# Adding beta on VectorE, an earlier request for raw weights, and a new order in the half tiles of a 1-core attention and mixture-of-experts kernel

## What is computed

```python
xn = _layernorm(x)
Q, K, V = xn @ Wq + bq, xn @ Wk + bk, xn @ Wv + bv        # 16 heads; Q and K have two halves of 64
A1, A2 = Q1 @ K1.T * s, Q2 @ K2.T * s                     # 512 x 512 for each batch and head
P = softmax(A1) - lam * softmax(A2)
Y = concat(P @ V) @ Wo + bo
attn = (layernorm(Y) * gamma + beta) * (1.0 - 0.8)
logits = t @ switch_w + switch_b                          # t: the 4096 tokens of xn; 8 experts
out = gelu(t @ w1[e] + b1[e]) @ w2[e] + b2[e]             # e = argmax of the logits, for each token
x = x + attn + out * max(softmax(logits))
```

## Time and profile before

| | |
|---|---|
| Median of 3 runs | 1838.65 us (1837.49 to 1839.98) |
| The profiled execution | 1841.33 us, of which the span of the trace is 1839.5 us |
| PE, DVE, ACT, POOL busy in the span | 97%, 84%, 77%, 36% |
| Front stage | to about 1465 us; PE full from 80 us on |
| Feed-forward stage | about 1465 to 1726 us; half tiles from 1652 us |
| Output stage | about 1726 us to the end |

### The profile page before, as it was taken

How to read it: one execution, slowest core, us unless ns; L and a number is a source line. 1 busy time by engine, 2 the same in 40 slices (tenths; PEclk the granted TensorE clock), 3 DMA queues, 4 the chain that set the end, 5 groups by cost and what they waited for, 6 DMA issues and landing times. The chain is left out here.

```text
span 1839.5 us, 32514 instructions
## 1 busy us (share of the span) xinstructions
PE 1789.6 (97%) x10474; PEld 1392.6 (76%) x10474; DVE 1538.1 (84%) x2636; ACT 1409.6 (77%) x3358; POOL 663.9 (36%) x717
## 2 busy tenths in 40 slices
PE   5999999999999999999999999999999999999997
PEld 4777777777777777777777777777677699999997
DVE  3988898899889888988898889888999866887467
ACT  4898888888888888888888888888788776676422
POOL 2444222222222222223222222222237455556554
PEclk8999999999999999999999999999999999999899
DMA  7899988888888888888888888888877586667698
GB/s 232 228 247 251 247 226 220 224 236 219 218 226 237 224 222 228 233 223 218 235 232 214 212 234 225 220 218 231 227 206 185 177 311 230 241 234 269 199 361 282
DMA packets 212915, 427.77 MB, mean 233 GB/s; under 512 B 28080, under 2 KB 107952, under 8 KB 206736
## 3 DMA queue, kind: packets, MB, share of 16 engines
q1 hardware_dynamic: 207744, 411.20, 80.1%
q0 software_dynamic: 4688, 13.51, 2.2%
q10 hardware_dynamic: 320, 1.05, 0.2%
HBM read 175.17 MB, written 49.15 MB: 122 GB/s over the span
## 5 line engine op out<-in xcount | busy, mean ns | idle before, releaser
L609 ACT ACTIVATE e<-p_score,nmax 128x512 f32<-128x512 f32 x1024 | 697.1, 688 | 134.1 <-DVE nmax L956 132.7
L475 POOL TENSOR_SCALAR e<-e,rrec,lam 128x512 f32<-128x512 f32 x512 | 394.0, 770 | 981.5 <-DVE rrec L923 981.0
L956 DVE TENSOR_REDUCE nmax<-p_score 128x2 f32<-128x1024 f32 x512 | 622.8, 1216 | 149.9 <-PE p_score L1101 145.8
L1101 PE MATMUL p_score<-ks,qs 128*128 128x512 f32 x2048 | 581.2, 406 | 13.8 <-ACT e L609 9.4
L1101 PEld LDWEIGHTS p_score<-ks,qs 128*128 128x128 f32 x2048 | 366.4, 189 | 184.6 <-issue 62.2
L1064 PE MATMUL p_proj<-xh,w 128*128 128x512 f32 x1024 | 386.2, 418 | 4.5 <-DVE xl L682 1.6
L930 DVE SCALAR_TENSOR_TENSOR pm<-e,rrec 128x512 f32<-128x512 f32 x512 | 382.8, 748 | 0.4 <-POOL e L475 0.2
L561 ACT COPY pT<-p_tr 128x512 f32<-128x512 f32 x512 | 301.7, 589 | 101.6 <-PE p_tr L1113 101.3
L1113 PE MATMUL p_tr<-consts,pm 128*128 128x128 f32 x2048 | 308.5, 273 | 1.7 <-ACT pT L561 1.6
L1113 PEld LDWEIGHTS p_tr<-consts,pm 128*128 128x128 f32 x2048 | 249.2, 140 | 80.2 <-issue 20.1
L1130 PE MATMUL p_pv<-pT,v 128*64 128x512 f32 x1024 | 247.7, 605 | 0.7 <-ACT pT L561 0.7
(11 more groups left out here) (211 smaller groups left out, 1832.9 us busy)
## 6 DMA issues: line engine op xcount, KB each, us to landing
ks<-k_parts SPq DMA_DIRECT2D x508, 256.0 KB, 4.8
qs<-q_parts SPq DMA_DIRECT2D x512, 128.0 KB, 4.3
w<-weight_parts_scratch SPq DMA_DIRECT2D x56, 1024.0 KB, 10.5
w<-in_w SPq DMA_DIRECT2D x46, 1024.0 KB, 7.1
oT_parts_scratch<-oT SPq DMA_DIRECT2D x32, 512.0 KB, 6.1
op<-oT_parts_scratch SPq DMA_DIRECT2D x32, 512.0 KB, 8.9
wv<-weight_parts_scratch SPq DMA_DIRECT2D x56, 256.0 KB, 5.5
weight_parts_scratch<-w SPq DMA_DIRECT2D x8, 1024.0 KB, 5.8
```

The source lines that it names most:

```text
L475: nc.gpsimd.tensor_scalar(e2, e2, rrec[:, g % 4, 1:2], lam[:, 0:1], ALU.mult, ALU.mult).then_inc(s_e2, 1)
L609: nc.scalar.activation(ex[:, g % EX, m, :], p_score[g % 2][:, m, :], ACT.Exp, bias=nmax[:, g % 2, m:m + 1], accum_out=rsum[:, g % 4, m:m + ...
L956: vec.tensor_reduce(nmax[:, g % 2, :], p_score[g % 2][:, :, :], AXX, ALU.max, negate=True).then_inc(s_max, 1)
L1101: last_op = nc.tensor.matmul(p_score[g % 2][:, m, :], qs[j][u][:, m, qt * P:(qt + 1) * P], ks[j][u][:, m, part, :], start=(part == 0), sto ...
```

## The change

It has five parts.

1. Start, PE: 12 and 8 transposes of a constant (`keep_warm`) before and after the first transposes of x. Nothing reads their results.
2. Start, DMAs: the spread of k0 of pair 0 is issued by two queues, map 0 by ACT and map 1 by SP, not all by ACT. SP asks for the raw weights of pair 2 right behind it, ahead of the spreads of the second head, and for the raw v of pair 3 behind those and ahead of the loads of x. These requests have waits that keep their order.
3. Start, ACT and POOL: `high_v(0)` stands before the first parts, `high_v(1)` before `scale_q(1)`; `high_v(2)` moves from step 0 to step 3, `low_v(2)` from step 1 to step 4.
4. Half tiles, DVE: in a half tile that has a next one, both `w1_high` of the next tile stand ahead of the four groups (`early`), not between them.
5. Output stage: SP asks for the parts of group 1 before those of group 2. DVE adds beta at the head of `base(n)`, behind a wait for x; POOL's `add_beta` is gone, so that POOL only gathers.

```diff
@@ -100,6 +100,7 @@
 PER_BATCH = S // GROUP
 X_PAIRS, X_STEP = (3, 5), 3
 MAGIC, NEWTON = 1597463007.0, 3
+WARM = (12, 8)
 LATER_STEPS = QT + 7 + 3 * NEWTON
 EX = 3
 WVC = 2 * P + NE
@@ -293,11 +294,11 @@
         xn_v = xn_d.rearrange("(n s p) e -> n p s e", s=2, p=P)
         HALF = KT * 2 * P
 
-        def spread_by(queue, u, what, pair):
+        def spread_by(queue, u, what, pair, maps=range(2)):
 
             j = pair % 2
             src = parts[what][u]
-            for m in range(2):
+            for m in maps:
                 a = src[m * D:(m + 1) * D]
                 if what == "q":
                     for part in range(2):
@@ -383,13 +384,17 @@
             sp.dma_start(swb[:, :], ins["swb"]).then_inc(s_bv, 16)
             sp.dma_start(bv[:, :], ins["bv"]).then_inc(s_bv, 16)
             spread(0, "q", 0)
+            sp.wait_ge(s_lo, 2)
+            spread_by(sp, 0, "k", 0, (1,))
+            sp.wait_ge(s_wvhi, 1)
+            load_raw_v(2)
+            load_raw(2)
             for what in "qk":
                 spread(1, what, 0)
+            sp.wait_ge(s_wvhi, 2)
+            load_raw_v(3)
             for n in range(PER_BATCH, 2 * PER_BATCH):
                 load_x(n)
-            load_raw(2)
-            for pair in (2, 3):
-                load_raw_v(pair)
             store_w(0)
             store_w(1)
 
@@ -473,7 +478,7 @@
                 if g == 0:
                     pool.wait_ge(s_lam, 1)
                 nc.gpsimd.tensor_scalar(e2, e2, rrec[:, g % 4, 1:2], lam[:, 0:1], ALU.mult, ALU.mult).then_inc(s_e2, 1)
-                if g == 1:
+                if g == 4:
                     low_v(2)
                 if st == 6 and pair + 3 < PAIRS:
                     low_v(pair + 3)
@@ -577,19 +582,19 @@
             for n in range(PER_BATCH):
                 x_high(n)
             high_qk(0, 1)
+            high_v(0)
             high_part(0, "q0")
             high_part(0, "k0")
             act.wait_ge(s_lo, 2)
-            spread_by(act, 0, "k", 0)
-            high_v(0)
+            spread_by(act, 0, "k", 0, (0,))
             act.wait_ge(s_sw, 16)
             nc.scalar.copy(wv[0][:, 0, :, 2 * P:WVC], sw[:, :, :]).then_inc(s_swhi, 1)
             high_part(0, "q1")
             high_part(0, "k1")
+            high_v(1)
             scale_q(1)
             high_qk(1, 0)
             high_qk(1, 1)
-            high_v(1)
 
             for g in range(STEPS):
                 pair, st = g // TPP, g % TPP
@@ -612,7 +617,7 @@
                 if g == EXP_STEP:
                     act.wait_ge(s_rd, SHIFTED)
                     nc.scalar.activation(exr[:, :, :], lg[:, :, :], ACT.Exp).then_inc(s_re, 1)
-                if g == 0:
+                if g == 3:
                     high_v(2)
                 if st == 5 and pair + 3 < PAIRS:
                     high_v(pair + 3)
@@ -1027,6 +1032,11 @@
             def group_pair(n):
                 return PAIRS * (n // PER_BATCH - 1) + X_PAIRS[n % PER_BATCH]
 
+            def keep_warm(count):
+
+                for _ in range(count):
+                    nc.tensor.transpose(p_tr[:, 0, :], ident, ident)
+
             def ranks():
                 pe.wait_ge(s_ones, 2)
                 pe.wait_ge(s_lo, 4 * (RANK_PAIR + 1) + 3)
@@ -1155,8 +1165,10 @@
                 last_op.then_inc(ahead.s_tr, 1)
 
             pe.wait_ge(s_const, 16)
+            keep_warm(WARM[0])
             for n in range(PER_BATCH):
                 transpose_x(n)
+            keep_warm(WARM[1])
             for what in ORDER:
                 project(0, what)
             for g in range(STEPS):
@@ -1454,8 +1466,8 @@
                 load_parts(0)
 
             turns(body, before_last=first_o)(sp)
+            load_parts(1)
             load_parts(2)
-            load_parts(1)
             load_whole(2)
             store(FFN_TILES - 1, 0, 1)
 
@@ -1498,11 +1510,6 @@
                 nc.gpsimd.tensor_tensor(w2p[j][:, 1, 0:f, :], w2[j][:, 0:f, :], w2p[j][:, 0, 0:f, :].bitcast(F32),
                                         ALU.subtract).then_inc(s_w2lo, 1)
 
-            def add_beta(n):
-                pool.wait_ge(s_x[n % R], 16 * (n // R + 1))
-                nc.gpsimd.tensor_tensor(x[n % R][:, :, :], x[n % R][:, :, :],
-                                        beta.unsqueeze(1).to_broadcast([P, 2, E]), ALU.add).then_inc(s_xb, 1)
-
             def fetch(n):
 
                 r = n % R
@@ -1515,16 +1522,10 @@
                         in_offset=bass.IndirectOffsetOnAxis(ap=slot_u[:, c:c + 1], axis=0)
                     ).then_inc(s_ff[r], 16)
 
-            pool.wait_ge(s_scaled, 1)
-            pool.wait_ge(s_w2lo_dve, 1)
-            for n in range(R):
-                add_beta(n)
             pool.wait_ge(s_st[0], 16 * (LOOPED // 2 + 1))
             pool.wait_ge(s_st[1], 16 * (LOOPED // 2))
             for n in range(GROUPS):
                 fetch(n)
-                if n >= R:
-                    add_beta(n)
 
         @block.scalar
         def _(act):
@@ -1650,6 +1651,10 @@
                         w1_high(2, 0, 1, k, False)
                     for k in range(KT):
                         w1_low(2, 0, k)
+                early = t.has(1) and t.exact and t.fs == 1
+                if early:
+                    for k in range(KT):
+                        w1_high(n + 1, 1 - j, t.half_next, k, False)
                 for g in range(HG):
                     dve.wait_ge(s_hhi, n * HG + g + 1)
                     if g == 0 and t.after(2):
@@ -1660,9 +1665,9 @@
                     if g == X_AT and t.x_in_middle():
                         x_low(n + 1, 1 - j, t.fs_next)
                     if t.has(1) and not t.first() and not t.second():
-                        if g < KT:
+                        if g < KT and not early:
                             w1_high(n + 1, 1 - j, t.half_next, g, not t.after(1))
-                        else:
+                        if g >= KT:
                             w1_low(n + 1, 1 - j, g - KT)
                 if t.has(1) and not t.x_in_middle():
                     x_low(n + 1, 1 - j, t.fs_next)
@@ -1724,6 +1729,9 @@
             def base(n):
 
                 r = n % R
+                dve.wait_ge(s_x[r], 16 * (n // R + 1))
+                v.tensor_tensor(x[r][:, :, :], x[r][:, :, :], beta.unsqueeze(1).to_broadcast([P, 2, E]), ALU.add
+                                ).then_inc(s_xb, 1)
                 dve.wait_ge(s_ff[r], 32 * (n // R + 1))
                 dve.wait_ge(s_xb, n + 1)
                 for s in range(2):
```

## The result

| | before | changed |
|---|---|---|
| Median | 1841.3 us (20 runs, 1837.5 to 1846.3) | 1845.24 us (20 runs, 1839.1 to 1849.4) |
| Profiled execution, its span | 1841.33, 1839.5 us | 1846.17, 1844.3 us |
| Ratio | | 1.0019, 95% interval 1.001 to 1.0027 |

What follows compares the result with a forecast made beforehand. It took the front to be held by DMA waits and the output stage by its bytes. Start -4.2, half tiles 0, output stage 0 - 0.7 + 1.0 made -3.9 from the median of 1838.65: 1834.7 us, range 1831.0 to 1838.3.

Steps and rivals of the forecast that it cites:

- The start: Front stage: earlier first work and weight loads were to make it sooner by 4.2 us, kept to the end.
- q0 at the upper level: Start: added transposes raise TensorE's clock, so q0's six matmuls are 0.23 us apart, 1.2 us won; bounds 0 and 1.2.
- no wait at `high_v(2)`: Start: ScalarE's wait of 9.08 us for the raw v of pair 2 was to be gone.
- the store as the wait that takes over: Start, `high_qk(2, 0)`: ScalarE waits for the store of pair 0's weights instead, some 6 us.
- Its landing: Start: the store of pair 0's weights lands at 39.7 us rather than 42.1; bounds 42.1 and 38.5.
- 33.4 at the latest: Start: the time in us by which ScalarE reaches the wait for the store of pair 0's weights.
- Half tiles: 0: Half tiles: the two moved casts are held up by GpSimd's subtraction, so nothing is won; at best 3.5 us.
- rival (b): Half tiles: the casts are not held up by GpSimd, 3.5 us more won, 1831.2 us; chance 0.09.
- The swap: Output stage, loads of groups 1 and 2: TensorE's wait moves from group 1 to group 3, 0; at best 2.0 us sooner.
- The adds: Output stage: VectorE's additions hidden in the turns, 2.2 us at the end against 2.9 us of GpSimd's hold-ups: -0.7.
- The gathers: Output stage: gathers of groups 14 and 15 go out a turn sooner, ahead of the last parts: +1.0, bounds 0 and 1.4.
- Rival (d): Output stage: VectorE's adds lie on the chain, each of six turns grows by up to 1.4 us, 1843.0 us; chance 0.08.

Runs made afterwards that it cites:

- part 4 alone: Kernel before with only both w1 casts moved ahead of the four groups in half tiles: 1848.14 us against 1840.59, ratio 1.003.
- held ones: GpSimd waits for a group's x before gathering for the next: kernel before with beta on VectorE, 1841.07 us; changed kernel without early w1 casts, 1836.07; before 1841.57.
- beta alone: Kernel before with beta added by VectorE and no addition by GpSimd, loads unswapped: 1840.04 us against 1840.59, ratio 0.999.

## Why the prediction failed, point by point

**The start.** Right, and a little too small. The steps came as written: q0 at the upper level, no wait at `high_v(2)`, the store as the wait that takes over. Its landing was put at 39.7 with bounds 38.5 and 42.1; the profiles show 38.3 to 42.0. ScalarE came to it later than "33.4 at the latest", at 35.5, so its wait was 3.44 us rather than some 6: the sum left out that ScalarE waits for VectorE's maxima, 1.41 and 0.43 us here. That changed nothing, as the landing decides. The gain was put at 4.2; it is 5.6 in the changed kernel's trace, where the store landed 0.7 us sooner than put and the maximum of step 5 followed 5.6 us behind it rather than 6.2, and 4.6 in the mean of all. One reading behind it was wrong: a DMA share of 0.95 doesn't mean that 5% is free, since the share passes 1 (1.08 in the output stage). From 20 to 40 us it is 1.06 in the changed kernel, at 298 GB/s after 259.

**"Half tiles: 0."** This is the step that failed: 0 with bounds -3.5 to 0, measured +8.5 in the trace and +7.6 in the median of part 4 alone. The lock, by which GpSimd and VectorE hold each other up, was reasoned rightly for the later tiles: "After GpSimd's end the same two casts, four `hp` and two `w1_low` are still to do". That holds as long as the second `w1_low` starts ahead of GpSimd's next subtraction. In the tile of the earlier trace rows and those beside it, it leads by 0.2 to 0.5 us; in tile 16 the two meet within 0.02 us. The trace of before shows that, at 1660.77 and 1660.79, but the prediction read the pattern of the later tiles and took it for all. So a loss had no place in the bounds. What the step should have said: who starts first here, by how much, and what it costs to be second: 4.4 us of waiting, 3 of them on TensorE, and then the clock.

The Trainium skill ("SBUF — State Buffer", SBUF: two separate sides) has the engine that starts first hold the ports that the two share for its whole instruction. The rows agree in both directions, 5.69 rather than 4.6 us for GpSimd when second and 5.58 rather than 1.21 for VectorE; but starts up to 0.03 us apart in the trace don't tell who was first. The prediction took from that page only that its rival (b) was unlikely, and not that the one instruction moved could come to lose.

**The output stage.** The swap: 0, right. The adds: -0.7 predicted, -0.51 measured; 2.1 rather than 2.2 for the additions, 2.6 rather than 2.9 for GpSimd's hold-ups. The gathers: right that they come ahead of what is waited for, but too small, and in the wrong place. They were put at +1.0 with bounds 0 to 1.4; between the casts of groups 2 and 15 it is 85.1 to 85.9 us in the four kernels where GpSimd adds (mean 85.3), and 86.5 to 87.4 in the eight where it gathers freely (mean 86.9): 1.5 in the mean and 1.82 here. The prediction had the gathers of groups 14 and 15 come ahead of the last parts. Instead the whole difference is there at the cast for group 9, which comes 46.2 to 47.1 us after that for group 2 where gathers wait (held ones too) and 47.8 to 48.7 us where they don't; from there to group 15 it is 38.3 to 39.1 us in all fourteen. By the cast for group 9, 17 gathers had gone out before and 20 in the changed kernel, and by that for group 15, 29 and 32. Three gathers of 128 KB at the 371 GB/s of the earlier trace rows make about 1.1 us, an estimate; what makes up the rest of the 1.8 isn't shown. Rival (d), that the adds lie on the chain, is refuted by the kernel without any.

The sum with the measured terms in place of the predicted ones: -5.6 + 8.5 + 0.5 + 1.8 - 0.5 = +4.7, against 4.8 between the spans (the +0.5 is from `hidden` of tile 22 to the cast for group 2, both at the lower clock). With the half tiles at 0 it would be -3.8, next to the forecast's -3.9: in part by luck, since the start gave 1.4 more than put and the gathers took 0.8 more. The one wrong term turned the sign.

## What to carry to other kernels

Where two engines contend for a lock, read for each place, not for the typical one, who starts first and by how much: an order that holds by hundredths of a microsecond is a cliff, and a wait put there on purpose, which here cost nothing, keeps it. Where the order is that close, a reordering that moves an engine's work by 0.1 us is to be costed with the full price of coming second, the idle time of TensorE and the clock behind it included. And an engine freed of work issues its DMAs sooner: in a stretch bound by its bytes they come ahead of what is waited for, 1.5 us in the mean here.

## What the hardware showed that was not expected

The clock fell, or did not, behind the same short gap. `hidden` of tile 22 begins 0.87 us late in the kernel before and in the one with beta alone, 58.27 and 58.29 us after that of tile 16. Timeline of TensorE, before and then the other:

```profile
1710.38 8.34 PE L1810 MATMUL p_h<-xsp,w1p 128*128 128x128 f32 x48 [0.87 <-issue]
```

```profile
1708.77 5.55 PE L1802 MATMUL p_h<-xsp,w1p 128*128 128x128 f32 x48 [0.87 <-issue]
```

In ten of the fourteen profiled executions this gap is 0.86 to 0.88 us. In five of them the 48 matmuls took 8.1 to 8.6 us, in the other five 5.55. To the cast for group 2 it is then 25.1 to 25.7 us in the six executions whose clock fell here, and 21.0 to 21.4 us in the eight whose clock didn't, with and without GpSimd's additions in both sets: 4 us by the clock. In four traces, that of the kernel without beta among them, the clock also fell in tile 19 or 20, which cost some 3 us each time. A good part of the spread of the runs, 1837 to 1846 us before, fits this: the slower runs have the lower mean clock. Behind the idle time of 2.9 to 3.0 us of the first half tile the clock fell in all three traces that have it.

The Trainium skill ("TensorE: Matmul & The Clock Gate", What's actually happening) says of a kernel's start that the moment of the clock's rise varies from run to run. With one trace of each kernel, no run here shows that; what varies in these traces is the fall, from kernel to kernel.
